# Reordering the prologue of the four attention layers: presets on the scalar engine, rope table first, late chunks projected outside the row maxima

## The reference

```
q = (x @ Wq), k = (x @ Wk), v = (x @ Wv)          # x normed
q, k = q*cos + rot(q)*sin, k*cos + rot(k)*sin      # a1 and a2 only
scores = q @ k.T / sqrt(hd)                        # causal mask in a1 and a2
out = softmax(scores) @ v
y = out @ Wo                                       # and, in f1 and f2, the experts
```

## Time and profile before

| | us |
|---|---|
| median of three runs | 3306.58 (3305.38 to 3307.19) |
| the profiled execution | 3307.29 |
| its span | 3305.6 |
| TensorE busy | 2887.2 (87%) |
| VectorE busy | 2313.2 (70%) |
| ScalarE busy | 1830.1 (55%) |
| GpSimd busy | 541.4 (16%) |
| TensorE's mean granted clock | 0.929 |

### The profile page before, as it was taken

How to read it: one execution, slowest core, us unless ns; L and a number is a source line. 1 busy time by engine, 2 the same in 40 slices (tenths; PEclk the granted TensorE clock), 3 DMA queues, 4 the chain that set the end, 5 groups by cost and what they waited for, 6 DMA issues and landing times. The chain is left out here.

```text
span 3305.6 us, 43798 instructions
## 1 busy us (share of the span) xinstructions
PE 2887.2 (87%) x15996; PEld 1098.8 (33%) x16044; DVE 2313.2 (70%) x3012; ACT 1830.1 (55%) x3749; POOL 541.4 (16%) x856
## 2 busy tenths in 40 slices
PE   5999989699999997699958999999987799876788
PEld 2444434122222223433321222222255233344345
DVE  5454555799999993566658999999926666563951
ACT  2215322388888885246634888888844266654012
POOL 0000000200010000222222000010003222231730
PEclk9999999699999999889977999999988799978979
DMA  3210121300000000311012000000000311000000
GB/s 111 93 49 1 36 87 52 116 21 18 19 19 19 18 11 28 91 40 38 33 44 105 18 19 19 19 19 20 23 14 26 90 35 47 28 8 24 0 0 13
DMA packets 67507, 121.71 MB, mean 37 GB/s; under 512 B 16082, under 2 KB 42707, under 8 KB 64124
## 3 DMA queue, kind: packets, MB, share of 16 engines
q1 hardware_dynamic: 67292, 118.90, 11.1%
HBM read 95.38 MB, written 23.48 MB: 36 GB/s over the span
## 5 line engine op out<-in xcount | busy, mean ns | idle before, releaser
L1250 DVE TENSOR_REDUCE arena<-ps 128x1 f32<-128x1024 f32 (+7 forms) x1536 | 1573.9, 1065 | 280.8 <-PE ps L894 185.1
L1122 ACT ACTIVATE arena<-ps 128x512 f32<-128x512 f32 (+3 forms) x2816 | 1382.6, 573 | 411.5 <-PE ps L957 350.4
L888 PE MATMUL ps<-arena 61*128 61x512 bf16 (+4 forms) x2816 | 946.6, 383 | 104.2 <-DVE arena L1250 40.2
L957 PE MATMUL ps<-arena 64*128 64x512 bf16 (+4 forms) x2768 | 736.3, 372 | 60.6 <-ACT arena L1122 33.0
L914 PE MATMUL ps<-arena 128*32 128x512 f32 (+3 forms) x5632 | 713.9, 579 | 0.6 <-POOL arena L1207 0.3
L957 PEld LDWEIGHTS ps<-arena 64*128 64x128 bf16 (+1 forms) x2816 | 206.3, 95 | 764.5 <-ACT arena L1122 537.1
L888 PEld LDWEIGHTS ps<-arena 61*128 61x128 bf16 (+1 forms) x2816 | 259.1, 96 | 439.8 <-DVE arena L1250 342.0
L337 PE MATMUL ps<-xnT,moe_up 128*128 128x512 f32 x480 | 232.4, 610 | 0.0
L453 ACT ACTIVATE arena<-ps 128x512 f32<-128x512 f32 x120 | 71.4, 597 | 224.9 <-PE ps L337 224.9
L523 DVE TENSOR_TENSOR arena<-arena,ps 128x512 f32<-128x512 f32 x120 | 82.2, 687 | 158.7 <-ACT arena L453 129.8
L1177 POOL TENSOR_TENSOR arena<-arena,ones 16x128 bf16<-16x128 f32 x96 | 42.8, 446 | 786.9 <-ACT arena L1107 778.7
(11 more groups left out here) (232 smaller groups left out, 2740.9 us busy)
## 6 DMA issues: line engine op xcount, KB each, us to landing
arena<-m_w SPq DMA_DIRECT2D x32, 512.0 KB, 3.4
arena<-f_q SPq DMA_DIRECT2D x60, 144.0 KB
arena<-f_k SPq DMA_DIRECT2D x180, 48.0 KB
arena<-m_w SPq DMA_DIRECT2D x64, 128.0 KB, 3.8
arena<-in_w SPq DMA_DIRECT2D x4, 2048.0 KB
arena<-a_q SPq DMA_DIRECT2D x14, 576.0 KB
arena<-a_k SPq DMA_DIRECT2D x42, 192.0 KB
a_q<-arena SPq DMA_DIRECT2D x44, 96.0 KB, 1.9
```

The lines of the kernel that those rows point to most:

```text
L888: last = nc.tensor.matmul(at[:, k0 // CHUNK, 0:n], score_rows(Qop[par], j, slice(q0, q0 + P)), score_rows(Kop[par], j, slice(k0, k0 + n)), ...
L957: nc.tensor.matmul(ps[:, ring_bank(item), off:CHUNK], shifted_rows(Kop[par], j, slice(kb * P, (kb + 1) * P)), shifted_rows(Qop[par], j, sl ...
L1122: nc.scalar.activation(pr[:, (at % 2) * 4 + j, off:CHUNK], ps[:, ring_bank(item), off:CHUNK], ACT.Exp).then_inc(s.ex, 1)
L1250: nc.vector.tensor_reduce(mq[:, half, j * 4 + qb:j * 4 + qb + 1], src, AXX, ALU.max).then_inc(s.sread, 1)
```

## The change

In f1, f2, a1 and a2 alike:

- The presets of `Qop`, `Kop` and `vx` (24 memsets of GpSimd and 12 of VectorE over the four layers) are now written by ScalarE in as many fills (`fill`: an ACTIVATE Copy of a broadcast column of ones with the value as scale), between its other work.
- The table DMA of a rope layer is issued ahead of the loads of the next layer's weights, and VectorE waits for the table after norming chunk 1 and not before.
- In f1 and f2 chunks 2 and 3 are projected, cut and their values made before the first score tile; TensorE now also waits for all 8 remainders there. In a1 and a2 chunk 2 is done before the first half of the maxima (TensorE waits for `rope` 6) and chunk 3 between the two halves. No work stands between reductions of one half.
- GpSimd makes the third parts of chunk 0 ahead of the deviation of chunk 3; in a1 and a2 the cut of the first maxima comes before the third parts of chunk 3, the copy of the first maxima on ScalarE ahead of chunk 3's `head`, and on SP the placing of the first maxima before the stores of chunks 2 and 3.
- Other PSUM banks take the projections.

```diff
-            def sync(sp):
+            def table(sp):
                 if rope:
                     sp.dma_start(tab, a[rope + "_tab"]).then_inc(s.tab, 16)
...
-                store_cut(2)
-                store_cut(3)
-                put_max(0, 0, 0)
+                if full:
+                    store_cut(2)
+                    store_cut(3)
+                    put_max(0, 0, 0)
+                else:
+                    put_max(0, 0, 0)
+                    store_cut(2)
+                    store_cut(3)
...
-            def proj_bank(ch, side):
+            def proj_banks(ch, side):
+                n = 2 * ch + side
                 if rope:
-                    return {1: 0, 2: 2}.get(2 * ch + side, PROJ)
-                return (2 if ch == 1 else PROJ) + side
+                    return {1: (0, 1), 2: (2, 3), 4: (0, 1), 5: (2, 3), 7: (TURNED, VALUES)}.get(
+                        n, (PROJ, PROJ + 1))
+                return ((PROJ, 2, PROJ, 0)[ch] + side,)
...
+                    if rope and n >= 3:
+                        pe.wait_ge(s.rope, (1, 2, 3, 4, 4)[n - 3])
+                    if rope and n == 7:
+                        pe.wait_ge(s.vcp, 3)
+                    if not rope and ch == 2:
+                        pe.wait_ge(s.rem1, side + 1)
...
-                pe.wait_ge(s.opsA, 16 * N_FIRST)
-                if rope:
-                    pe.wait_ge(s.rope, 4)
+                project(2, 0)
+                project(2, 1)
                 if full:
+                    norm_tensor(pe, s, 3, TURNED)
+                    project_values(2)
+                    project(3, 0)
+                    project(3, 1)
+                    project_values(3)
+                    pe.wait_ge(s.opsA, 16 * N_FIRST)
                     pe.wait_ge(s.ops0, placed(0))
+                    pe.wait_ge(s.rem1, 2 * CHUNKS)
+                else:
+                    project_values(2)
+                    norm_tensor(pe, s, 3, TURNED)
+                    pe.wait_ge(s.opsA, 16 * N_FIRST)
+                    pe.wait_ge(s.rope, 6)
                 for k in range(16):
                     scores(-1, 0, 0, k)
-                    if k in (3, 5):
-                        project(2, k // 4)
-                    if k == 6:
-                        project_values(2)
-                        norm_tensor(pe, s, 3, TURNED)
-                    if k in (8, 10):
-                        project(3, k // 10)
-                    if k == 12:
-                        project_values(3)
+                if not full:
+                    project(3, 0)
+                    project(3, 1)
                 turn_max(0, S_SLOT)
+                if not full:
+                    project_values(3)
...
+                def fill(to, value):
+                    n = to.shape[1]
+                    return nc.scalar.activation(to, ones[:, 0:1].to_broadcast([P, n]), ACT.Copy, scale=value)
+
+                def preset(par):
+                    fill(words(Qop[par]), 0.0)
+                    fill(words(Kop[par]), MINUS_ONES).then_inc(s.kneg, 1)
...
                 copy_turned(0)
+                preset(0)
                 for ch in range(CHUNKS):
+                    if ch == 3 and not full:
+                        first_max()
                     head(ch)
-                    if ch < 2:
+                    if ch + 1 < CHUNKS:
                         copy_turned(ch + 1)
                     middle(ch)
                     copy_values(ch)
-                    if ch == 2:
-                        copy_turned(3)
+                    if ch == (1 if full else 0):
+                        preset(1)
+                    if ch == (3 if full else 2):
+                        for par in range(3):
+                            fill(vx[par].rearrange("p k j c -> p (k j c)"), 1.0).then_inc(s.vset, 1)
+                        preset(2)
+                if full:
+                    first_max()
...
-                for g in range(CHUNKS):
+                for g in range(3):
                     norm_gpsimd(pool, s, t, g, double)
-                    if g == 1:
-                        preset(0)
                 third_part(0)
+                norm_gpsimd(pool, s, t, 3, double)
                 third_part(1)
-                preset(1)
                 third_part(2)
-                third_part(3)
-                cut_max(0, 0)
-                preset(2)
+                if full:
+                    third_part(3)
+                    cut_max(0, 0)
+                else:
+                    cut_max(0, 0)
+                    third_part(3)
...
                 norm_chunk(dve, s, t, x_rows, 0)
+                norm_chunk(dve, s, t, x_rows, 1)
                 if rope:
                     dve.wait_ge(s.tab, 16)
-                norm_chunk(dve, s, t, x_rows, 1)
                 cutting(0)
                 norm_chunk(dve, s, t, x_rows, 2)
                 cutting(1)
                 norm_chunk(dve, s, t, x_rows, 3)
...
-                for par in range(3):
-                    nc.vector.memset(vx[par], 1.0).then_inc(s.vset, 1)
-                maxima(0, 0, between)
+                cutting(2)
+                if full:
+                    cutting(3)
+                maxima(0, 0)
+                if not full:
+                    cutting(3)
                 maxima(0, 1)
```

47 lines of the change are left out of this document (19 added, 28 removed).

## The result

The changed kernel takes 3254.3 us (median of 4 runs, 3251.5 to 3258.6), the kernel before 3306.6 us (4 runs, 3305.4 to 3307.2). The ratio is 0.9846, 95% interval 0.9834 to 0.9858: 52 us less, where 48.5 was forecast. The profiled execution took 3254.6 us with a span of 3252.5.

What follows compares the result with a forecast made beforehand. VectorE's reductions were taken to bound the first halves in f1 and f2, a projection-rotation-projection chain in a1 and a2. Savings 8.2 + 7.3 + 16.5 + 16.5 = 48.5 us from 3306.6 gave 3258 us, range 3244 to 3275.

Steps and rivals of the forecast that it cites:

- The halves themselves: First halves of f1 and f2: with nothing between reductions they shrink to 18.8 us, saving 6.7 and 5.8 us.
- Their start in f: First score tile of f1 and f2: operands land earlier as third parts precede chunk 3's deviation, 1.5 us gained each.
- thin cover: f1 and f2: chunk 3's remainders ready about 592.4, 0.8 us ahead of the operands; beyond it, lateness costs one for one.
- The walk of a1 and a2: a1 and a2 prologues, followed step by step from chunk 2's copy to the second half's start: 16.5 us saved each.
- The fills at no price: ScalarE's fills, estimated at 1.04 and 1.91 us, fall within its waits and cost nothing.
- D: Rival, chance 0.02: ScalarE's fills at k times their estimate delay `head`; the whole change turns slower from about k = 3.
- unfavourable end: Fills at 2.2 us per 1024 columns, twice the estimate: about 2 us lost per f layer, 5 per a layer.
- The stores' cover of 5 us: a1 and a2: stores of chunks 2 and 3 land near 1400.5, 5 us before ScalarE's first loop instruction at 1405.3.
- the prediction's own sign: Stated test: the forecast is wrong if, among other signs, ScalarE's first exponential waits for a DMA.
- B: Rival, chance 0.12: all moved projections run at half clock, 7.5 instead of 5.8 us a group, 6.8 us less gain, 3265.
- C: Rival, chance 0.14: the late chain outlasts the operands in f1 and f2; total gain 28 to 42 us, 3264 to 3278.
- E: Rival, counted within the forecast's 0.66: in f operands land no earlier and the half keeps gaps; 3261 us.

Runs made afterwards that it cites:

- e11: The changed kernel unedited, run again beside the kernel with the Q operand's load in three DMAs: 3253.0 us, ratio 0.984.
- e5: The changed kernel with GpSimd norming chunk 3 ahead of chunk 0's third parts again, as before: 3264.9 us, ratio 0.9878.
- e6: The changed kernel with every ScalarE fill cut into 8 pieces: 3262.2 us, ratio 0.987.
- e2: The changed kernel with the presets back on GpSimd as memsets and the fills of vx back on VectorE: 3269.2 us, ratio 0.9894.
- e4: The kernel before with only the table's load issued first and chunk 1 normed ahead of the wait for it: 3303.1 us, ratio 0.9992.
- e7: The changed kernel with SP, in a1 and a2, issuing chunk 2's stores, the maxima, unit 1's operands' load, then chunk 3's stores: 3258.0 us, ratio 0.9861.
- e8: The changed kernel with SP, in a1 and a2, issuing chunk 2's stores, the maxima, chunk 3's stores, and unit 1's operands' load last: 3269.7 us, ratio 0.9891.
- e9: The changed kernel with a unit's Q operand load in a1 and a2 issued as three DMAs of 24 rows: 3251.3 us, ratio 0.9839.

## Why the prediction was right, step by step

**The halves themselves** (6.7 and 5.8 us in f): measured 6.6 and 5.7. That VectorE's reductions bound them, at half clock too, is shown by the rows.

**Their start in f** (1.5 us each): 2.4 and 1.9, and 1.7 and 2.0 in e11. This term was somewhat under-sized. I counted the two GpSimd instructions of chunk 3's deviation and not the wait ahead of them for VectorE; e5 gives 2.4 and 1.8 for this order alone. The thin cover of 0.8 us was 1.9 in one execution and 0.8 in the other.

**The walk of a1 and a2** (16.5 each): 16.7 and 17.4 at the start of the second half. Its steps in a1, after the layer's start, forecast and measured: projections of chunk 2 begin 19.6 and 19.5; maxima 28.9 and 28.2; their end 37.5 and 37.0; second half 45.8 and 45.65.

**The fills at no price**: held at the estimated length. With half again the work (e6) it still held in three layers, and in f1 the thin cover went, 2 us. The working was not consistent here: rival D's formula charges an f layer 4.2k - 2.2, that is 2.0 us at the estimate itself (k = 1) and 6.2 at twice it, where the sum charges nothing and the unfavourable end about 2; the measured starts in f side with the sum. I had put the gain of taking memsets off GpSimd at 3.5 us in a1 and worked no number for a2; e2 gives 5.7 and 6.8 at the second halves, `vx` included, of which 3.2 and 4.1 are left at the first exponential, and e4 a second place where it counts.

**The stores' cover of 5 us**: the step that failed. "SP: maxima placed near 1390.7" is 47.5 us after the layer's start; it was 54.6. It left the maxima's store and load the 1.8 us apart that they were before, when the operands' load was issued over 22 us ahead of them. Freed of the threading, the maxima come 9.3 us behind the operands' load, and the round trip is 8.7 us. The cover was eaten and 1.8 and 2.0 us of the gain of a1 and a2 went with it. By the prediction's own sign ("if ScalarE's first exponential waits for a DMA") the forecast was wrong in this step, though its sum was not. e7 shows the load as cause, e8 how long it takes, e9 that splitting it gives the wait back.

**The sum**: 48.5 forecast, 47.0 by stages, 52.3 by medians (50.7 in e11). That 47.0 is so near is partly luck: 2.4 us more than forecast had been gained at the second halves, and 3.8 went to the stores. The 5 us between stages and medians lie outside the prologues, most of them in a stretch that varies by that much from one execution to the next.

**Rivals.** B would have cost 6.8 us: both moved groups of a1 ran partly at half and partly at full clock (granted clock 0.69 and 0.62 on average), 5.4 and 5.85 us. The Trainium skill, "TensorE: Matmul & The Clock Gate", section "Why this matters for your kernels", has gaps bring the half clock. Chunk 2's group, with 3.43 us idle ahead of it, agrees; chunk 3's started at half clock though TensorE had not idled over 1.1 us at a time since chunk 2's. C did not occur in the changed kernel; e6 brought it about in f1. D's condition, fills at three times the estimate, is refuted by 1.07 and 1.92 us. The prediction took k = 3 from the rule of the Trainium skill named beside it, "ScalarE: Activation LUTs", section "Rules for kernel authors", that plain arithmetic belongs on VectorE, and said that no row compared the two on a fill. The trace of the kernel before had one: VectorE's memsets of `vx` (128x1024 in f32) took 0.91 us each, where ScalarE's fill of the same size takes 1.07. No run put the presets on VectorE; what counted here was which engine was idle and which neighbour it disturbed. E is refuted by the starts in f, 2.4 and 1.9 us earlier.

## To carry to other kernels

Work threaded into a stretch to fill gaps can make the stretch as long as the threaded chain: compare the stretch with the busy time of its bound engine, and if another wait nearby is long enough, put the work there. When a change draws two DMA issues closer together, price the small one by what is in flight ahead of it, not by its own time from a trace in which the queue was empty. If a large load moves slowly while the share of DMA engines is low, try to split it before reordering the queue; here that gave the wait back where the orders tried did not, though not yet a gain that the whole time shows.

## What the runs showed of the hardware that I had not expected

From issue to landing a store of 12 KB took 1.4 us with nothing large ahead of it in the queue (e7), 8.7 behind a load of 1.1 MB issued 9 us earlier, and 14.4 behind one issued 3 us earlier (e5). That load kept 2.8 of 16 DMA engines busy (e8). The Trainium skill, "DMA: Bandwidth & Descriptors", section "Why a DMA increments its semaphore by 16 and not by 1", gives the number of engines as the largest up to 16 that divides the outermost dimension of both sides, 3 for a load whose source repeats itself three times. The share agrees, and so does what splitting it did: 0.60 of the engines' time instead of 0.13 in its first 3.4 us (e9).

Four VectorE norming instructions that alone take 1.1 us took 4.1 beside two GpSimd memsets (e4), 2.8 beside two GpSimd TENSOR_TENSORs, and 6.3 beside all four (e2); in each case they ended within 0.7 us of the end of those GpSimd instructions.
